# The last seven up-sampled pieces: TensorE adds shortcut and rows in PSUM, with separate banks for the last halves

## The reference

```python
def forward(x, ...):
    shortcut = x
    out = bilinear_resize(x, H // 2, W // 2)
    out = relu(bn(conv1x1(out, conv1_w), bn1_s, bn1_b))
    out = att(out, q_w, q_b, k_w, k_b, v_w, v_b, att_gamma)   # softmax attention over all 64*64 pixels
    out = relu(bn(out, bn2_s, bn2_b))
    out = bn(conv1x1(out, conv2_w), bn3_s, bn3_b)
    out = bilinear_resize(out, H, W)
    return relu(out + shortcut)
```

## Time and profile before

| | |
|---|---|
| median of 3 runs | 2601.41 us (2600.03 to 2603.33) |
| profiled execution | 2600.95 us |
| its span, first to last instruction | 2599.1 us |
| TensorE busy | 2310.5 us (89%) |
| VectorE busy | 2137.8 us (82%) |
| POOL busy | 1594.8 us (61%) |
| ScalarE busy | 1545.2 us (59%) |
| mean granted TensorE clock | 0.97 |

### The profile page before, as it was taken

The page is one execution under the profiler, slowest core; times in us unless marked ns, Lnnn a source line. Parts: engine busy times, 40 slices in busy tenths (PEclk is TensorE's granted clock), DMA queues, the critical chain, the costliest instruction groups (busy, mean ns, idle before and its releaser), DMA issues.

```text
span 2599.1 us, 53215 instructions
## 1 busy us (share of the span) xinstructions
PE 2310.5 (89%) x15914; PEld 1634.2 (63%) x15914; DVE 2137.8 (82%) x3357; ACT 1545.2 (59%) x2753; POOL 1594.8 (61%) x1537
## 2 busy tenths in 40 slices
PE   2389999899999999989999999989999999999981
PEld 1157776666747666666747666666665777666660
DVE  8977778888677888888777888878867888888879
ACT  1136666666746666666755666656664666666662
POOL 6854038878824888878833888777880344444475
PEclk8689999999999999999999999999999999999995
DMA  5312002222301222222210222222220111111123
GB/s 169 113 49 66 1 25 97 90 81 97 114 17 58 99 98 97 85 95 97 98 42 33 98 98 95 92 92 87 98 82 1 66 66 65 65 65 66 65 98 129
DMA packets 59188, 204.59 MB, mean 79 GB/s; under 512 B 8736, under 2 KB 9824, under 8 KB 58976
## 3 DMA queue, kind: packets, MB, share of 16 engines
q1 hardware_dynamic: 40544, 135.26, 16.1%
q10 hardware_dynamic: 18432, 67.12, 6.3%
HBM read 135.24 MB, written 67.11 MB: 78 GB/s over the span
## 4 chain that ended last, share of the span: by engine, by line
POOL 33%; issue 26%; PE 23%; DVE 12%; POOLq 4%; ACT 1%; DVEq 0%; DMA 0%; ACTq 0%; SPq 0%
POOL ct L343 5%; PE acc L968 5%; PE acc L970 4%; PE acc L969 4%; POOL xin L306 4%; POOL rt L331 3%; POOL cd L338 3%; POOL rd L326 3%; POOL dd L314 3%; POOL xin L310 3%; POOL y L336 3%; PE et L846 3%; POOL xin L308 2%; POOL dd L312 2%; PE acc L894 2%
## 5 line engine op out<-in xcount | busy, mean ns | idle before, releaser
L968 PE MATMUL acc<-vh,ph 128*128 128x257 f16 x4096 | 1122.4, 274 | 31.1 <-DVE pl L638 29.2
L970 PE MATMUL acc<-vh,pl 128*128 128x257 f16 x4096 | 1118.0, 273 | 0.0
L969 PE MATMUL acc<-vl,ph 128*128 128x256 f16 x4096 | 1112.9, 272 | 0.0
L416 ACT ACTIVATE ph<-et 128x512 f16<-128x512 f32 x1024 | 608.7, 594 | 578.3 <-PE et L846 560.6
L638 DVE TENSOR_TENSOR pl<-et,ph 128x512 f16<-128x512 f32 x1024 | 698.4, 682 | 104.7 <-ACT et L417 77.9
L417 ACT ACTIVATE et<-et 128x512 f32<-128x512 f32 x1024 | 606.4, 592 | 0.0
L614 DVE TENSOR_REDUCE mx<-emx 128x1 f32<-128x512 f32 x632 | 433.3, 686 | 176.9 <-PE emx L834 168.0
L969 PEld LDWEIGHTS acc<-vl,ph 128*128 128x128 f16 x4096 | 401.8, 98 | 276.2 <-issue 23.0
L968 PEld LDWEIGHTS acc<-vh,ph 128*128 128x128 f16 x4096 | 401.0, 98 | 106.0 <-DVE pl L638 38.3
L846 PE MATMUL et<-qs,ks 98*128 (+1 forms) x1024 | 392.2, 383 | 68.7 <-DVE pl L638 67.3
L970 PEld LDWEIGHTS acc<-vh,pl 128*128 128x128 f16 x4096 | 396.3, 97 | 56.6
(11 more groups left out here) (111 smaller groups left out, 2546.2 us busy)
## 6 DMA issues: line engine op xcount, KB each, us to landing
xres<-in_x SPq DMA_DIRECT2D x146, 512.0 KB, 4.2
out<-xres ACTq DMA_DIRECT2D x128, 512.0 KB, 2.6
xin<-in_x SPq DMA_DIRECT2D x110, 512.0 KB, 3.6
osb<-in_L_conv_conv_w SPq DMA_DIRECT2D x1, 256.0 KB, 7.7
osb<-in_L_conv_v_w SPq DMA_DIRECT2D x1, 256.0 KB, 7.6
hbuf<-in_L_conv_conv_w SPq DMA_DIRECT2D x1, 256.0 KB, 7.6
ident<-identity SPq DMA_DIRECT2D x1, 64.0 KB, 7.8
uw<-up_weights SPq DMA_DIRECT2D x1, 64.0 KB, 2.5
```

What stands on the lines that cost most here:

```text
L416: ops.activation(ph[:, t % 4, :], et[t % 2][:, :], ACT.Exp)
L968: mm(acc[it][:, 0:C + 1], ph[:, tt % 4, pt], vh[:, tt, 0:C + 1], start=tt == 0, stop=False)
L969: mm(acc[it][:, 0:C], ph[:, tt % 4, pt], vl[:, tt, :], start=False, stop=False)
L970: last = mm(acc[it][:, 0:C + 1], pl[:, tt % 4, pt], vh[:, tt, 0:C + 1], start=False, stop=tt == JT - 1)
```

## The change

**What it does.**
- Block 31 takes eight pieces (113 to 120) instead of six: piece j of them is added in steps 4j+1 to 4j+4, the eighth in steps 29 and 30, ahead of the row sums.
- `y2` and `ct` get two buffers. In all blocks POOL's chain of piece u waits for the additions of piece u - 2, no longer of u - 1.
- After block 31 the second half's transposes go to the bank `emx` and the halves of `conv2` to `et[0]` and `et[1]`, so that no half waits for the other's bank.
- Seven late pieces, 121 to 127, remain. For each, TensorE adds shortcut and doubled rows in two of the `acc` banks: a matmul with the identity over `xres` (`start=True`) and one over `y2`, each value read twice (`start=False`), for each half of the rows; four float32 matmuls of 512 columns per piece. VectorE then makes one addition per half, bank plus `ct` into `xres` (two additions per piece instead of four). The pairs of banks alternate.
- POOL has the chains of 121, 124, 125, 127, VectorE those of 122, 123, 126, now with two sets of buffers. The additions come in the order 121, 122, 124, 123, 125, 126, 127, and `LATE_STEPS` interleaves them with VectorE's chains.

The diff, cut to its core:

```diff
-        y2 = sb("y2", [P, UR, S])
+        y2 = sb("y2", [P, 2, UR, S])
...
         cd = sb("cd", [P, UR, S + 1])
-        ct = sb("ct", [P, UR, S, 2])
...
             if is_last(b, c):
                 for j in range(PIECES, PIECES + MORE_LAST):
-                    yield j, (NB * B - 1) * PIECES - 11 + j, b, n - 2, (n - 2) % 2, (1 + j) % PIECES
+                    u = (NB * B - 1) * PIECES - 11 + j
+                    yield j, u, b, u // PIECES - (B - 1) * NB, u // PIECES % 2, u % PIECES
...
+        def late_y_rdy(u):
+
+            chunk, k = divmod(u, PIECES)
+            return 2 * min(NB * B - 1, chunk + k // 2) + k % 2 + 1
...
+        late_buffers = []
+        for d in range(2):
+            free = xr[:, d * (NB // 2):(d + 1) * (NB // 2)].rearrange("p k h r c -> p (k h r c)")
+            sizes = [(UR // 2 + 1) * S, UR * S, UR * S, UR * (S + 1), 2 * UR * S]
+            at = [sum(sizes[:i]) for i in range(5)]
+            rd_, rt_, y2_, cd_, ct_ = (free[:, o:o + z] for o, z in zip(at, sizes))
+            late_buffers.append((
...
-            at_least(eng, up_v, added * 2)
+            at_least(eng, *y2_free)
...
-            at_least(eng, up_added, added * 2)
+            at_least(eng, *ct_free)
...
-                        if j == 3:
+                        if j == (5 if is_last(b, c) else 3):
                             pool.wait_ge(y_rdy, g * 2)
-                        u = ups[j][0]
-                        up_piece(*ups[j], u * UP, u)
+                        u, un, pr, k = ups[j]
+                        up_piece((j + 1) % 2, un, pr, k, u * UP, (up_v, (u - 1) * 2), (up_added, (u - 1) * 2))
...
-            before = LATE
             for i, u in enumerate(LATE_POOL):
                 _, _, un, pr, k = late_piece(u)
-                if u == LATE_POOL_LAST_CHUNK:
-                    pool.wait_ge(y_rdy, 2 * NB * B)
-                up_piece(u, un, pr, k, (LATE + i) * UP, before)
-                before = LATE + LATE_ORDER.index(u) + 1
+                pool.wait_ge(y_rdy, late_y_rdy(u))
+                if i < 2:
+                    y2_free, ct_free = (up_v, (LATE + i - 1) * 2), (up_added, (LATE + i - 1) * 2)
+                else:
+                    o = LATE_ORDER.index(LATE_POOL[i - 2])
+                    y2_free, ct_free = (late_x, 2 * o + 2), (up_added, (LATE + o + 1) * 2)
+                up_piece((LATE + i) % 2, un, pr, k, (LATE + i) * UP, y2_free, ct_free)
...
-                cv = wrk[:, :].rearrange("p (r c) -> p r c", c=S)
+                cv = bank[:, :].rearrange("p (r c) -> p r c", c=S)
...
-                bn3(NB * B - 1, (NB - 1) % 2, half, False, True)
+                bn3(NB * B - 1, (NB - 1) % 2, half, False, True, et[half])
...
-                    residual(b * NB + (NB - 1), NB - 1, half)
+                    last = isinstance(b, int) and b == B - 1
+                    residual(b * NB + (NB - 1), NB - 1, half, (wrk, emx)[half] if last else wrk)
...
+            def late_chain(u):
+
+                d = LATE_DVE.index(u)
+                _, _, un, pr, k = late_piece(u)
+                dve.wait_ge(y_rdy, late_y_rdy(u))
+                y2_free = (late_x, 2 * LATE_ORDER.index(LATE_DVE[d - 2]) + 2) if d > 1 else (late_v, 2)
+                up_chain(dve, ops, late_v, 2 + d * UP, un, pr, k, late_buffers[d % 2], y2_free, (late_v, 2))
+
+            def late_add(u):
+
+                i = LATE_ORDER.index(u)
+                s = xslot(late_piece(u)[0])
                 if u in LATE_POOL:
-                    dve.wait_ge(up_p, (LATE + LATE_POOL.index(u) + 1) * UP)
-                    y2_c, ct_c = y2, ct
+                    k = LATE_POOL.index(u)
+                    dve.wait_ge(up_p, (LATE + k + 1) * UP)
+                    t = ct[:, (LATE + k) % 2]
                 else:
-                    dve.wait_ge(y_rdy, 2 * min(NB * B, u // PIECES + (2 if k > 1 else 1)))
-                    dve.wait_ge(late_v, done)
-                    up_chain(dve, ops, late_v, done, un, pr, k, buffers, LATE + i)
-                    done += UP
-                    dve.wait_ge(late_v, done)
-                    y2_c, ct_c = buffers[2], buffers[4]
-                for part in range(4):
-                    add_part(j, u, part, LATE + i, y2_c, ct_c)
+                    d = LATE_DVE.index(u)
+                    dve.wait_ge(late_v, 2 + (d + 1) * UP)
+                    t = late_buffers[d % 2][4]
+                for r in range(2):
+                    rs = slice(r * (UR // 2), (r + 1) * (UR // 2))
+                    dve.wait_ge(late_x, 2 * i + r + 1)
+                    ops.tensor_tensor(xres[:, s, rs, :], acc[2 * (i % 2) + r][:, :].rearrange("p (r c) -> p r c", c=H),
+                                      t[:, rs].rearrange("p r c two -> p r (c two)"), ALU.add).then_inc(up_added, 1)
+
+            for d in range(2):
+                ops.memset(late_buffers[d][3], 0.0).then_inc(late_v, 1)
+            for what, i in LATE_STEPS:
+                (late_chain if what == "chain" else late_add)(LATE + i)
...
-                if half:
+                if half and bank is wrk:
...
-                if half:
+                if half and bank is wrk:
...
-                out_transposes(NB * B, half)
+                out_transposes(NB * B, half, (wrk, emx)[half])
             for half in range(2):
-                conv2(NB * B - 1, half)
+                conv2(NB * B - 1, half, et[half])
+            for i, u in enumerate(LATE_ORDER):
+                s = xslot(late_piece(u)[0])
+                banks = acc[2 * (i % 2):2 * (i % 2) + 2]
+                if i > 1:
+                    pe.wait_ge(up_added, (LATE + i - 1) * 2)
+                pe.wait_ge(xres_ld[s], (u - s) * 4 + 16 * (XRES_FIRST[s] + 1))
+                rows = [slice(r * (UR // 2), (r + 1) * (UR // 2)) for r in range(2)]
+                for r in range(2):
+                    mm(banks[r][:, :], ident[:, :], xres[:, s, rows[r], :].rearrange("p r c -> p (r c)"), start=True, stop=False)
+                if u in LATE_POOL:
+                    k = LATE_POOL.index(u)
+                    pe.wait_ge(up_p, (LATE + k) * UP + 3)
+                    y = y2[:, (LATE + k) % 2]
+                else:
+                    d = LATE_DVE.index(u)
+                    pe.wait_ge(late_v, 2 + d * UP + 3)
+                    y = late_buffers[d % 2][2]
+                for r in range(2):
+                    mm(banks[r][:, :], ident[:, :], y[:, rows[r], :].unsqueeze(3).broadcast_to([P, UR // 2, S, 2]),
+                       start=False, stop=True).then_inc(late_x, 1)
...
-MORE_LAST = 2
+MORE_LAST = 4
 T_CV_LAST = (12, 14)
-T_ADD_LAST = ((1, 3, 4, 5), (7, 8, 9, 10), (11, 12, 13, 14), (20, 21, 22, 23), (25, 26, 27, 28), (30, 30, 31, 31))
-T_RELU_LAST = (6, 11, 16, 24, 29)
+T_ADD_LAST = tuple((i, i + 1, i + 2, i + 3) for i in range(1, 29, 4)) + ((29, 29, 30, 30),)
+T_RELU_LAST = (5, 9, 13, 17, 21, 25, 29)
 LATE = PIECES * (NB * B - 1) - 11 + PIECES + MORE_LAST
-LATE_ORDER = tuple(LATE + i for i in (0, 2, 1, 4, 3, 6, 5, 8, 7))
-LATE_POOL = tuple(LATE + i for i in (0, 1, 3, 5, 7))
-LATE_POOL_LAST_CHUNK = PIECES * (NB * B - 1) - 2
-assert sorted(LATE_ORDER) == list(range(LATE, PIECES * NB * B)) and LATE_POOL_LAST_CHUNK in LATE_POOL
+LATE_ORDER = tuple(LATE + i for i in (0, 1, 3, 2, 4, 5, 6))
+LATE_POOL = tuple(LATE + i for i in (0, 3, 4, 6))
+LATE_DVE = tuple(LATE + i for i in (1, 2, 5))
+LATE_STEPS = (("chain", 1), ("add", 0), ("chain", 2), ("add", 1), ("add", 3), ("chain", 5), ("add", 2), ("add", 4),
+              ("add", 5), ("add", 6))
```

More of the change, by code:

```diff
@@ L422, in relu_h, with bn3 @@
                                scale=par[:, S2, half:half + 1]).then_inc(h_rdy, 1)
-            def bn3(chunk, par_, half, first, last):
+            def bn3(chunk, par_, half, first, last, bank=wrk):
                 act.wait_ge(cv_rdy, chunk * 2 + (half + 1))
@@ L773, in leave @@
                 for half in range(2):
-                    residual(b * NB + (NB - 1), NB - 1, half)
+                    last = isinstance(b, int) and b == B - 1
+                    residual(b * NB + (NB - 1), NB - 1, half, (wrk, emx)[half] if last else wrk)
             walk(dve, enter, blk, leave, last_apart=True)
-            free = xr[:].rearrange("p k h r c -> p (k h r c)")
-            sizes = [(UR // 2 + 1) * S, UR * S, UR * S, UR * (S + 1), 2 * UR * S]
-            at = [sum(sizes[:i]) for i in range(5)]
@@ L783, in _ @@
-            rd_, rt_, y2_, cd_, ct_ = (free[:, o:o + z] for o, z in zip(at, sizes))
-            cd_ = cd_.rearrange("p (r c) -> p r c", c=S + 1)
-            buffers = (rd_.rearrange("p (r c) -> p r c", c=S), rt_.rearrange("p (r two c) -> p r two c", two=2, c=S),
-                       y2_.rearrange("p (r c) -> p r c", c=S), cd_, ct_.rearrange("p (r c two) -> p r c two", two=2, c=S))
-            ops.memset(cd_, 0.0).then_inc(late_v, 1)
-            done = 1
-            for i, u in enumerate(LATE_ORDER):
-                j, _, un, pr, k = late_piece(u)
+            def late_chain(u):
```

(19 more changed lines are left out.)

24 lines of the change are left out of this document (14 added, 10 removed).

## The result

The changed kernel took **2606.65 us** (median; 2602.85 to 2610.3), the kernel before, beside it on the same chip, 2601.18 (2599.17 to 2606.59): ratio 1.0019, 95% interval 1.001 to 1.0028. Forecast were 2593.5 us and a range to 2598.5. The change is slower by about 5 us, just short of the 0.2% that the prediction set as its border, and the time lies outside the range.

The account below looks back on a forecast made before the run. The prediction took TensorE to bound the blocks and VectorE the tail behind block 31. Its steps put the last Relu at 2588.2 instead of 2595.98, 7.8 us less: 2593.2, plus 0.46 for the median, rounded to 2593.5 us; range 2586 to 2598.5.

Parts of the forecast that it names:

- Two buffers: All blocks: POOL may run a piece ahead; costed at nothing, bounds -3 to +3 us.
- TensorE is what covers this: Blocks before 31: TensorE hides VectorE's lengthened additions; if cover fails over 30 blocks at 0.1 us each, 3 us.
- Block 31 with eight pieces: Block 31: POOL sets the pace; row sums come at 2530.1 instead of 2529.29, 0.8 us later.
- 7.65 near the unhindered one: Block 31: time in us per POOL chain for pieces 118 to 120, against 7.2 unhindered and 9.05 with waits.
- The last halves: After block 31's row sums: conv2 halves follow one another, the second bn3 ending at 2543.4, 4.1 us earlier.
- VectorE's tail: After block 31: chains of 8.8 us and PSUM additions of 0.61 put the end of piece 123's additions at 2571.4.
- The rule on slow PSUM sources: Tail additions: 120 cycles fixed cost from PSUM against 58 from SBUF, 0.5 us more for eight additions on the path.
- The load of piece 127: Tail: it waits for piece 123's slot, so it lands at 2579.1, with no cover now.
- TensorE's last four matmuls: Tail's end: after about 4 us idle the clock has just fallen; they take 7.3 us, last Relu at 2588.2.
- The rival: Tail's end: the clock holds through the last gap, everything ends 3.6 us earlier, 2589.9; chance 0.28.
- the one that let block 31 grow: Block 31: chains of 9.05 us or stalled pl put row sums at 2534, forecast 2597.5; chance 0.12.
- a matmul at half speed: Tail: the matmul reading each y2 value twice streams at half speed at the lower clock, about 2623; chance 0.05.

Follow-up runs that it names:

- the waits alone: The kernel before with two buffers and the shorter waits in blocks 0 to 31, nothing else of the change: 2609.92 us, ratio 1.0033.
- shorter chains: Changed kernel, old waits before block 31, POOL's column products there covering half the columns (rest not computed): single run, 2593.42 us, block 31 59.06.
- column waits put back: Changed kernel, before block 31 POOL's column products wait again for all column additions, row waits stay short: 2591.79 us, ratio 0.9965.

## Why the prediction was wrong

Worked from the ends in the two profiled executions, the last `Relu` was forecast at 2588.2 and came at 2597.95, 9.75 us later: 8.7 from the first step, 6.6 from the second, less 5.5 from the tail.

- ***Two buffers.* Failed, and this decides the sign:** with the old waits before block 31 the same kernel is faster than the one before (0.9989, 0.998 to 0.9998). "Elsewhere nothing waits on what is made earlier: I cost it at nothing", with 3 us either way for the additions that it lengthens. Measured +8.7, and some 14 us for the column waits alone. The step looked for who waits on POOL. The price lay in what POOL's own waits did: they kept its column products off VectorE's column additions. The earlier trace rows had the sign of it, a maximum of 1750 ns against a median of 684, and the text read it; it bounded the effect at 0.1 us a block, and it was 0.3 in the changed kernel and 0.4 with the waits alone. "TensorE is what covers this" was wrong as well: the 452 additions before block 31 took 8.0 us longer and the stretch 8.8 us.
- ***Block 31 with eight pieces.* Failed on the term "7.65 near the unhindered one" and on where piece 118 starts.** The last three chains took 8.7 us each without any wait (2514.28 to 2540.31), 3.1 us more than forecast. The row of 7.2 us had no addition beside it; the 9.05 of the next chain less its two waits of 0.69 is 7.67, but without the waits additions lie beside the chain. And the forecast let piece 118 start when `bn3` of block 30 releases it, 29.3 us behind that block's end; it started 33.3 us behind it, released by nothing but POOL's own chains before, 4.0 us more. It counted three chains, where eight at 8.5 are 68 us for a block that had taken 57. Seven pieces and shorter chains show it: 57.23 and 59.06 instead of 64.76.
- ***The last halves.* Right in mechanism, near nothing in worth alone.** `bn3` ends 13.3 us behind the row sums, as forecast (2543.4 - 2530.1); the separate banks alone gain 0.5 us.
- ***VectorE's tail.* Right in the main.** The earlier trace rows were misread in one place: VectorE did not run without a gap from the row sums before, it waited 1.27 us for the second half's transposes (at 2535.11); no term of the sum rests on it. The first half of `win` came 10.5 us behind the row sums (10.0 forecast), piece 123's additions were done 39.5 behind them (41.3): chains of 8.0 to 8.2, not 8.8. PSUM additions started 0.60 apart, as the short value said. The rule on slow PSUM sources that the prediction had set beside it (the Trainium skill, VectorE: DVE Perf Modes, section on the TRN2 errata) shows no effect: 1.27 us for two from PSUM, 1.28 or 1.29 for two from SBUF in the run with the additions on VectorE.
- ***The load of piece 127.* Right:** 2584.85 to 2592.45 is 7.6 us, forecast 7.7. It was also the tail's largest loss, which the order of two steps could take away (4.7 us).
- ***TensorE's last four matmuls.* The rival was right in this execution, by luck.** The clock held over 3.84 us of waiting (3.67 us for the sum, not 7.3), which is 3.6 of the 5.5 us by which the tail was shorter than forecast. Two executions with the same tail went the other way: behind gaps of 3.82 us (old waits before block 31) and 3.90 us (column waits put back) the clock stood at 0.50 at first, and the sum took 5.1 and 5.3 us. The forecast for the lower level, 7.3, was over-sized too: 6.6 us was the longest such sum in any run.

So the rivals were placed in the wrong stretch, all but the one that let block 31 grow. The only one on the losing side was a matmul at half speed; that POOL, a piece ahead, would slow the engine that it feeds was bounded away. What stays open: in the last image the changed kernel's pair of additions is as long as before (0.841 + 0.870 against 0.711 + 0.998 us) and its six blocks still take 1.7 us more; and why the row wait gains nothing there once the column wait is short is read off the lengths, not tried.

## What to carry to other kernels

A wait that guards a buffer may also be what keeps the instructions of two engines apart that slow each other. Before shortening one, ask which instructions will run side by side without it, take each pair's long case from the trace (here 1.4 to 1.5 us for an addition of 0.68), count them in every block, and try each wait by itself and both together: here one gained 6 us, the other lost some 8, and with both the gain was gone. And where a step packs more work into a stage, divide the stage by the busiest helper's rate with company beside it, not by its best.

## What the runs showed of the hardware

- POOL's and VectorE's instructions that overlap are both longer: 0.68 to 1.47 us for VectorE's addition, 2.55 to 3.00 for POOL's two products. POOL's chain of seven instructions took 7.2 us with no addition beside it and 8.5 on average with VectorE's additions beside all of it.
- A float32 matmul whose moving operand reads each value twice (innermost stride 0) took as long as a plain one: 1.88 us for four instructions of 512 columns.
- VectorE's additions of two SBUF operands took 1.02 us on average beside a POOL instruction and 0.68 alone; its subtraction of the same size with one operand in PSUM took 0.68 in both cases.
- The length of TensorE's idle gap alone did not say whether its clock stayed up. In the changed kernel it kept the upper level over 3.84 us of waiting for the load; with the old waits before block 31, in the same tail, it had fallen to the lower one after 3.82 us, and with seven pieces and the order of the change after 3.13 us:

```profile
2585.53 3.36 PE L1049 MATMUL acc<-xres,ident 128*128 128x512 f32 x4 [3.82 <-DMA xres<-in_x]
```

```profile
2580.59 3.75 PE L1049 MATMUL acc<-xres,ident 128*128 128x512 f32 x4 [3.13 <-DMA xres<-in_x]
```
